# Attention with row maxima: one bank and 512 score columns per exponential, three banks for scores by key, four for scores by query

## Chip, cores and metric

One NeuronCore of a Trainium2 chip runs the whole program. The metric is device time in microseconds (us) of one execution. The profile is of one execution; its span is 2486.1 us, and that execution took 2487.8 us in all.

## What is computed

The reference is one small hybrid network over 2 sequences of 1024 tokens with 128 channels. In order: a wide attention with low-rank updates, an expert layer, a narrow attention (16 heads of 8 channels), an expert layer, a narrow attention over a window, then twice an attention with an expert layer behind it, with a recurrent mixing layer between the two. The change touches three of these parts, in which a softmax subtracts a true row maximum. The first (the window stage here) is

```python
for start in range(0, S, W):                       # W = 128
    scores = einsum('bhqd,bhkd->bhqk', wq, wk) * scale   # wk, wv: keys 0..end
    scores = where(mask, neg, scores)
    attn = softmax(scores, axis=-1)
    outs.append(einsum('bhqk,bhkd->bhqd', attn, wv))
```

and the other two (the causal blocks) are

```python
att = einsum('bhqk' of q, k) / sqrt(hd)
att = where(causal, att, -inf)
att = softmax(att, axis=-1)
y = einsum('bhqk,bhkd->bhqd', att, v)
```

each with 16 heads of 8 channels over 1024 tokens and 2 sequences. (In the first, the mask is counted from key 0 in every block, so the query at place r of a block sees keys 0 to r alone: one tile of 128 keys for all queries.) The narrow attention before them (the clipped one) needs no maximum.

## The kernel before

`four_heads` (L540) runs all four narrow attentions. It takes four heads at a time (8 groups `g` for 2 sequences of 16 heads) and, inside a group, units `(side, kt, c0)`: 512 queries of one side against 128 keys, of which queries before `c0` are cut off by causality. A causal block has 12 units per group: on side 0 widths 512, 384, 256, 128 (kt 0 to 3), on side 1 five of width 512 (kt 0 to 4), then 384, 256, 128. The window stage has 2 units per group, each 512 wide. The argument `use_max` is true for the window stage and the two blocks, and false for the clipped attention.

Per unit, TensorE computes *scores by key* (keys on partitions, queries in columns; `cols`, L681) into PSUM, ScalarE takes the exponential into `probs` (L878, or L874 for a unit at most 256 wide), GpSimd cuts the diagonal (L906), and TensorE multiplies with the values (`values`, L706, two units later: LAG) into bank 7, which ScalarE evicts at the end of a side (L826). The four heads sit in two row groups of the array: heads 0 and 2 on partitions 0 to 63, heads 1 and 3 on 64 to 127, so matmuls of heads i and i+1 run beside each other.

The row maxima come from a second computation, *scores by query* (`score_pair`, L723; mask matmuls L747), which VectorE reduces (`tensor_reduce`, L949). These are the row jobs: 38 per group in a block, issued two at a time. Their maxima are split into three bf16 parts (L849 to L851), turned by TensorE (L785), and loaded by DMA as extra rows of the q stack (L641), so that scores by key come out with the maximum subtracted. The jobs of a group run during the group before it.

PSUM has 8 banks of 512 fp32 columns. With `use_max`: scores by key have banks 0 to 3 as two pairs (`pairs = 2`). One *visit* is two banks, one head in each, 2 x (512 - c0) columns, and one exponential reads it. `cols` of visit n waits until the exponential of visit n-2 is done (L690, L691). A unit over 256 wide has two visits (heads 0, 1 and heads 2, 3), any other one. Banks 4, 5, 6 are a ring for row jobs, turns and the final transposes ("divide", L790): job n waits until job n-3 was read (L727), and as row jobs go in pairs, a pair waits for the first job of the pair before it. Bank 7 holds the outputs. Without `use_max` there are three pairs and one ring bank.

TensorE works in order. Each step s of the loop at L803 is: `cols(U, 0)`, side work of place 0, `values(U - 2)`, side work of place 1, `cols(U, 1)` (where the unit has two visits), side work of place 2. `side_jobs` (L484) places the row jobs: `column_costs` (L473) gives each place a cost, and pairs of jobs are spread evenly over the sum of the costs; so they move only if the costs do. Before the first unit of a stage, step 0 holds the row jobs that must come first.

## Time and profile before

| | us |
|---|---|
| device time, median of 3 runs | 2486.44 (2483.86 to 2488.78) |
| the profiled execution | 2487.8 |
| its span | 2486.1 |
| TensorE matmul busy | 2002.9 (81%) |
| VectorE busy | 1605.0 (65%) |
| ScalarE busy | 1411.4 (57%) |
| GpSimd busy | 876.8 (35%) |

The time is the device time of the whole program. The span runs from the first to the last instruction that the profile holds. Busy times are averages over stages that have different limits. The changed stages lie, in the profiled execution, from about 1410 to 1509 us (window stage), 1545 to 1820 us (first block) and 2059 to 2333 us (second block). TensorE's busy time is modelled from its starts, and each run of matmuls is shown with about 0.18 us of pipeline behind its last column.

### The profile page before, as it was taken

The page shows a single profiled execution, that of the slowest core. Times are in us where ns is not written, and L with a number is a line of the kernel's source. Part 1 is how long each engine was busy: PE and PEld are TensorE (multiplying, and loading weights), DVE is VectorE, ACT ScalarE, POOL GpSimd, SP SyncE. Part 2 cuts the span into 40 slices and gives each one's busy share as a digit, 9 for nine tenths or more (in the row PEclk, how much of TensorE's full clock was granted, in tenths as well). Part 3 has the DMA queues.
Part 4 walks back from the last instruction along what each step waited for, and adds up shares of the span by engine and source line. Part 5 has one row for each costly group of instructions (what it writes and reads, how often), then busy time and mean ns, then how long its engine had stood idle before and what let it go on. Part 6 is the DMA issues. An engine that isn't in the chain of part 4 may idle for free. (4 is left out here: it accounts for less than half of the span.)

```text
span 2486.1 us, 37698 instructions
## 1 busy us (share of the span) xinstructions
PE 2002.9 (81%) x13700; PEld 1132.1 (46%) x13700; DVE 1605.0 (65%) x3423; ACT 1411.4 (57%) x2024; POOL 876.8 (35%) x624
## 2 busy tenths in 40 slices
PE   4999999999999944758836786688879744888798
PEld 2666666666666632622322533122247631222367
DVE  5887787887877546651156464788723685888324
ACT  3777776777778643269852244266753152566641
POOL 3887776877768400242201103122200023121100
PEclk8999999999999966969957888599989865899899
DMA  2000000000000040062050121211010002210100
GB/s 78 1 5 1 3 5 1 1 3 5 1 3 1 1 157 16 2 161 59 11 173 1 51 54 59 74 32 32 17 35 1 1 17 66 74 37 17 35 1 18
DMA packets 55936, 81.37 MB, mean 33 GB/s; under 512 B 13434, under 2 KB 21706, under 8 KB 55626
## 3 DMA queue, kind: packets, MB, share of 16 engines
q1 hardware_dynamic: 55754, 78.96, 11.4%
q8 instruction: 112, 1.84, 0.3%
q14 instruction: 70, 0.57, 0.1%
HBM read 58.85 MB, written 19.33 MB: 31 GB/s over the span
## 5 line engine op out<-in xcount | busy, mean ns | idle before, releaser
L878 ACT ACTIVATE probs<-psum_banks 128x1024 f32<-128x1024 f32 (+1 forms) x416 | 384.2, 981 | 254.9 <-PE psum_banks L695 209.1
L1305 POOL TENSOR_SCALAR l0a_rows<-l0a_rows,l0a_rinv 128x1024 f32<-128x1024 f32 x160 | 454.3, 2844 | 188.2 <-DVE l0a_rinv L1267 184.6
L949 DVE TENSOR_REDUCE neg_max<-psum_banks 128x1 f32<-128x512 f32 (+3 forms) x672 | 415.2, 661 | 136.4 <-PE psum_banks L747 107.3
L1255 DVE TENSOR_REDUCE l0a_nmax<-psum_banks 128x1 f32<-128x1024 f32 x256 | 312.4, 1220 | 140.0 <-PE psum_banks L1149 138.1
L1201 ACT ACTIVATE l0a_rows<-psum_banks,l0a_nmax 128x1024 f32<-128x1024 f32 x256 | 285.8, 1116 | 60.8 <-DVE l0a_nmax L1255 59.3
L718 PE MATMUL psum_banks<-probs,v_ones 128*32 128x512 f32 (+3 forms) x2432 | 265.3, 518 | 7.3 <-POOL probs L906 3.7
L1163 PE MATMUL psum_banks<-packed,l0a_rows 128*128 128x128 f32 x2048 | 267.1, 273 | 2.0 <-POOL l0a_rows L1305 0.9
L1148 PE MATMUL psum_banks<-l0a_kh,l0a_qw 128*128 128x512 f32 x512 | 242.7, 474 | 21.6 <-POOL l0a_qw L1294 13.7
L1163 PEld LDWEIGHTS psum_banks<-packed,l0a_rows 128*128 128x128 f32 x2048 | 239.2, 141 | 42.3 <-issue 4.8
L740 PE MATMUL psum_banks<-k_stack,q_stack 56*128 56x128 bf16 (+3 forms) x1024 | 145.0, 336 | 123.6 <-DVE neg_max L949 91.6
L906 POOL TENSOR_SCALAR_AFFINE_SELECT probs<-probs 128x512 f32<-128x512 f32 x192 | 123.2, 647 | 330.4 <-ACT probs L878 279.9
L695 PE MATMUL psum_banks<-q_stack,k_stack 59*128 59x512 bf16 (+7 forms) x1216 | 177.1, 344 | 65.5 <-ACT probs L878 33.5
L1149 PE MATMUL psum_banks<-l0a_kl,l0a_qw 128*128 128x512 f32 x512 | 205.3, 401 | 0.0
L740 PEld LDWEIGHTS psum_banks<-k_stack,q_stack 56*128 56x128 bf16 x1024 | 48.5, 98 | 292.8 <-DVE neg_max L949 257.8
L1148 PEld LDWEIGHTS psum_banks<-l0a_kh,l0a_qw 128*128 128x128 f32 x512 | 97.9, 191 | 144.1 <-ACT l0a_rows L1201 77.1
L1876 DVE SCALAR_TENSOR_TENSOR l1f_y<-psum_banks,rt_g,l1f_y 128x128 f32<-128x128 f32 x256 | 72.1, 344 | 103.5 <-PE psum_banks L1814 103.5
L1222 DVE SCALAR_TENSOR_TENSOR l0a_ts<-psum_banks,l0a_sin 32x512 f32<-32x512 f32 x192 | 131.9, 687 | 4.2
L1838 ACT ACTIVATE l1f_h<-psum_banks 128x512 f32<-128x512 f32 x128 | 75.6, 598 | 102.6 <-PE psum_banks L1800 102.3
L1196 ACT ACTIVATE x_norm<-psum_banks 128x512 f32<-128x512 f32 x128 | 76.1, 595 | 98.0 <-PE psum_banks L1163 97.8
L695 PEld LDWEIGHTS psum_banks<-q_stack,k_stack 59*128 59x128 bf16 (+1 forms) x1216 | 50.4, 95 | 177.2 <-ACT probs L878 111.1
L433 POOL TENSOR_SCALAR l1f_y<-x_res,ln_mv,ln_rstd 128x128 f32<-128x128 f32 x32 | 25.9, 820 | 297.9 <-DVE ln_rstd L404 297.9
L1175 PE MATMUL psum_banks<-x_norm,l0a_v 128*64 128x512 f32 x512 | 124.0, 604 | 6.0 <-ACT l0a_ot L1206 6.0
(292 smaller groups left out, 3361.2 us busy)
## 6 DMA issues: line engine op xcount, KB each, us to landing
q_stack<-q_parts SPq DMA_DIRECT2D x116, 96.0 KB
k_stack<-k_eight SPq DMA_DIRECT2D x28, 224.0 KB
qkv<-in_l0f_w SPq DMA_DIRECT2D x6, 1024.0 KB, 5.5
k_eight<-parts SPq DMA_DIRECT2D x22, 256.0 KB
moe_b<-in_l0f_b SPq DMA_DIRECT2D x32, 128.0 KB, 3.6
k_stack<-k_eight SPq DMA_DIRECT2D x16, 256.0 KB
l1f_w<-in_l1f_w SPq DMA_DIRECT2D x16, 256.0 KB
k_eight<-first_parts SPq DMA_DIRECT2D x14, 256.0 KB
```

The source lines that it names most:

```text
L695: m = pe.matmul(PS[:, bank, to], S.Kst[stack(i), slot(g, i), kt * P:(kt + 1) * P], S.Qst[stack(i), slot(g, i), side * HALF + c0:(side + 1) ...
L718: m = pe.matmul(PS[32 * i:32 * (i + 1), 7, c0:HALF], S.Vx[:, NT * b + kt, h0 + i, :], S.Pt[:, U % PBUFS, i, c0:HALF], start=kt == 0, stop= ...
L740: last[heads] = pe.matmul(bank[:, at:at + k1 - k0], S.Qst[rows, slot(g, i), jq * P:(jq + 1) * P], S.Kst[rows, slot(g, i), k0:k1], start=fi ...
L878: act.activation(S.Pt[:, U % PBUFS, 2 * half:2 * half + 2, c0:HALF], PS[:, bank:bank + 2, c0:HALF], ACT.Exp).then_inc(exp_done, 1)
L949: dve.tensor_reduce(out, scores, AX, ALU.max, negate=True).then_inc(job_read, 1)
L1148: pe.matmul(scores(s)[:, c0:c0 + HALF], q, R.Kh[:, b, c0:c0 + HALF], start=True, stop=False)
L1149: m = pe.matmul(scores(s)[:, c0:c0 + HALF], q, R.Kl[:, b, c0:c0 + HALF], start=False, stop=True)
L1163: m = pe.transpose(PS[:, 4 + a, jj * P:(jj + 1) * P], R.Pr[:, (NT * ps + 2 * jj + a) % RING, kt * P:(kt + 1) * P], S.ident[:])
L1201: act.activation(R.Pr[:, s % RING, :], scores(s), ACT.Exp, bias=R.nmax4[:, s % 4:s % 4 + 1], accum_out=R.rsum4[:, s % 4:s % 4 + 1]).then_i ...
L1222: ins = dve.scalar_tensor_tensor(R.t_sin[to, u % 3, :], PS[src, bank_of(job), :], scale_of(job), R.sinT[src, job[2] % 2 * HALF:(job[2] % 2 ...
L1255: dve.tensor_reduce(R.nmax4[:, s % 4:s % 4 + 1], scores(s), AX, ALU.max, negate=True).then_inc(max_done, 1)
L1305: rows_divided.mark(pool.tensor_scalar(R.Pr[:, s % RING, :], R.Pr[:, s % RING, :], R.rinv4[:, s % 4:s % 4 + 1], None, ALU.mult))
```

## The change

With `use_max`, scores by key now take banks 0, 1, 2 one at a time, and the ring has banks 3, 4, 5, 6. A visit is now one bank with two heads of one row group (0 and 2, or 1 and 3) side by side in it, up to 256 queries each, so at most 512 columns, and one exponential reads it. `visits_of` lists them: a 512-wide unit has four visits (queries 0 to 255 of heads 0, 2; the same of heads 1, 3; then queries 256 to 511 of each), a 384-wide unit two of 512 columns and two of 256, a 256-wide unit two of 512, a 128-wide unit two of 256. TensorE issues two visits at once, so that the two row groups still work beside each other: `cols(U, v0, v1)` of visits n and n+1 waits for the exponential of visit n-2 (`exp_done` at n-1, for three banks). The first matmul in a bank has start set, the second head's does not. The eviction of the outputs by ScalarE stands behind the first visit of a unit, as it did before. `column_costs` follows the new visits: a 384-wide unit has costs 512 before and 256 after the values, where it had 384 and 384. Without `use_max` nothing changes.

```diff
--- before.py
+++ after.py
@@ -470,14 +470,22 @@
             [(kind, (i,), j) for kind, j in (("full", 4), ("full", 5), ("three", 6), ("full", 6), ("full", 7), ("tail", 7)) for i in range(4)])
 
 
+def visits_of(unit, use_max):
+
+    c0, half = unit[2], HALF // 2
+    if not use_max:
+        return [((0, 1, 2, 3), c0, HALF)] if HALF - c0 <= half else [((0, 1), c0, HALF), ((2, 3), c0, HALF)]
+    cuts = list(range(c0, HALF, half)) + [HALF]
+    return [(heads, q0, q1) for q0, q1 in zip(cuts, cuts[1:]) for heads in ((0, 2), (1, 3))]
+
+
 def column_costs(units):
 
     shape_change = 460
     costs = []
     for side, kt, c0 in units:
-        w = HALF - c0
-        cols = [2 * w, 0] if w <= HALF // 2 else [w, w]
-        costs.append((cols[0], 4 * w + shape_change, cols[1]))
+        streamed = [q1 - q0 for _, q0, q1 in visits_of((side, kt, c0), True)]
+        costs.append((sum(streamed[:2]), 4 * (HALF - c0) + shape_change, sum(streamed[2:])))
     return costs
 
 
@@ -554,7 +562,7 @@
     turn_at = {e: k for k, e in enumerate(turns)}
     first, second = row_jobs(nk)
     last_rows = {e: number["rows", e[1], (second if second and e[2][-1] else first)[-1]] for e in turns}
-    pairs, ring = (2, (4, 5, 6)) if use_max else (3, (6,))
+    in_flight, ring = (3, (3, 4, 5, 6)) if use_max else (3, (6,))
     products_of, rows_of_stack, per_batch = (56, 59, 160) if use_max else (64, 64, 176)
     parts_of_q = ((0, 3), (24, 3), (48, 1)) if use_max else ((0, 3), (24, 3), (48, 2))
     per_group = 16 * 2 * (1 + len(parts_of_q))
@@ -586,14 +594,20 @@
 
         return 16 * sum(transfers_of_c(f) for f in turns[:turn_at[e] + 1] if f[1] % SLOTS == e[1] % SLOTS)
 
-    def narrow(U):
-
-
-        return HALF - units[U % nu][2] <= HALF // 2
+    def pieces(U):
+        return visits_of(units[U % nu], use_max)
 
     visits = [0]
     for U in range(total):
-        visits.append(visits[-1] + (1 if narrow(U) else 2))
+        visits.append(visits[-1] + len(pieces(U)))
+
+    def scores_of(n, visit):
+        heads, q0, q1 = visit
+        w = q1 - q0
+        if use_max:
+            return {i: PS[:, n % in_flight, k * w:(k + 1) * w] for k, i in enumerate(heads)}
+        return {i: PS[:, 2 * (n % in_flight) + i % 2, q0:q1] if len(heads) == 2 else
+                PS[:, 2 * (n % in_flight) + i % 2, i // 2 * w:(i // 2 + 1) * w] for i in heads}
 
     with phase(S, 28) as (block, sems):
         (cols_ready, exp_done, masked, pv_done, evicted, job_ready, job_read, split_done, c_split, c_copied,
@@ -678,30 +692,33 @@
 
         @block.tensor
         def _(pe):
-            def cols(U, h):
-                (g, u), n = divmod(U, nu), visits[U] + h
-                side, kt, c0 = units[u]
-                if h == 0 and u == 0:
+            def cols(U, v0, v1):
+                (g, u), n = divmod(U, nu), visits[U] + v0
+                side, kt, _ = units[u]
+                at_once = [(scores_of(visits[U] + v, pieces(U)[v]), pieces(U)[v]) for v in range(v0, v1)]
+                if v0 == 0 and u == 0:
                     pe.wait_ge(loaded[g % SLOTS], per_group * (g // SLOTS + 1))
-                if h == 0 and use_max and kt == 0:
+                if v0 == 0 and use_max and kt == 0:
                     pe.wait_ge(c_loaded[g % SLOTS], c_landed(next(e for e in turns if e[1] == g and side in e[2])))
                     if U == 0:
                         pe.wait_ge(ones_set, 32)
-                if n >= pairs:
-                    pe.wait_ge(exp_done, n - pairs + 1)
-                for i in range(2 * h, 4 if narrow(U) else 2 * h + 2):
-                    bank = 2 * (n % pairs) + i % 2
-                    to = slice(i // 2 * (HALF - c0), (i // 2 + 1) * (HALF - c0)) if narrow(U) else slice(c0, HALF)
-                    m = pe.matmul(PS[:, bank, to], S.Kst[stack(i), slot(g, i), kt * P:(kt + 1) * P],
-                                  S.Qst[stack(i), slot(g, i), side * HALF + c0:(side + 1) * HALF], start=True,
-                                  stop=tri != "window", skip_group_check=True)
+                if n + v1 - v0 > in_flight:
+                    pe.wait_ge(exp_done, n + v1 - v0 - in_flight)
+                last = {}
+                for k in range(len(at_once[0][1][0])):
+                    for v, (to, (heads, q0, q1)) in enumerate(at_once):
+                        i = heads[k]
+                        last[v] = pe.matmul(to[i], S.Kst[stack(i), slot(g, i), kt * P:(kt + 1) * P],
+                                            S.Qst[stack(i), slot(g, i), side * HALF + q0:side * HALF + q1],
+                                            start=k == 0 or not use_max, stop=tri != "window", skip_group_check=True)
                 for r in range(2 if tri == "window" else 0):
-                    for i in range(2 * h, 2 * h + 2):
-                        rows = stack(i, 64)
-                        m = pe.matmul(PS[:, 2 * (n % pairs) + i % 2, :].rearrange("p (n c) -> p n c", c=P), S.behind[rows, r, :],
-                                      S.before[rows, r, :].unsqueeze(1).to_broadcast([64, 4, P]), start=False, stop=r == 1,
-                                      skip_group_check=True)
-                m.then_inc(cols_ready, 1)
+                    for v, (to, (heads, q0, q1)) in enumerate(at_once):
+                        rows, bank = stack(heads[0], 64), PS[:, (n + v) % in_flight, 0:2 * (q1 - q0)]
+                        last[v] = pe.matmul(bank.rearrange("p (n c) -> p n c", c=P), S.behind[rows, r, :],
+                                            S.before[rows, r, :].unsqueeze(1).to_broadcast([64, 2 * (q1 - q0) // P, P]),
+                                            start=False, stop=r == 1, skip_group_check=True)
+                for v in last:
+                    last[v].then_inc(cols_ready, 1)
 
             def values(U):
                 g, u = divmod(U, nu)
@@ -802,8 +819,10 @@
 
             for s, places in enumerate(steps):
                 U = s - 1
-                if 0 <= U < total:
-                    cols(U, 0)
+                once = 2 if use_max else 1
+                of_step = range(0, len(pieces(U)) if 0 <= U < total else 0, once)
+                for v in of_step[:1]:
+                    cols(U, v, v + once)
                 side_work(places[0])
                 if use_max and 0 <= U - LAG < total:
                     values(U - LAG)
@@ -811,8 +830,8 @@
                     values(U - LAG - 1)
                     values(U - LAG)
                 side_work(places[1])
-                if 0 <= U < total and not narrow(U):
-                    cols(U, 1)
+                for v in of_step[1:]:
+                    cols(U, v, v + once)
                 side_work(places[2])
 
         def evict(eng, V):
@@ -862,21 +881,26 @@
                 U = s - 1
                 if use_max and U in second_batch:
                     parts(second_batch[U])
-                for half in range(1 if U < total and narrow(U) else 2):
+                for v, visit in enumerate(pieces(U)) if U < total else [(0, None)]:
                     if U < total:
-                        side, kt, c0 = units[U % nu]
-                        if U >= PBUFS and half == 0:
+                        heads, q0, q1 = visit
+                        if U >= PBUFS and v == 0:
                             act.wait_ge(pv_done, U - PBUFS + 1)
-                        n = visits[U] + half
+                        n = visits[U] + v
                         act.wait_ge(cols_ready, n + 1)
-                        bank = 2 * (n % pairs)
-                        if narrow(U):
-                            act.activation(S.Pt[:, U % PBUFS, :, c0:HALF].rearrange("p (h a) c -> p a h c", a=2),
-                                           PS[:, bank:bank + 2, 0:2 * (HALF - c0)].rearrange("p a (h c) -> p a h c", h=2),
+                        w, bank = q1 - q0, 2 * (n % in_flight)
+                        if use_max:
+                            act.activation(S.Pt[:, U % PBUFS, heads[0]:heads[-1] + 1:2, q0:q1],
+                                           PS[:, n % in_flight, 0:2 * w].rearrange("p (h c) -> p h c", c=w),
                                            ACT.Exp).then_inc(exp_done, 1)
-                            continue
-                        act.activation(S.Pt[:, U % PBUFS, 2 * half:2 * half + 2, c0:HALF], PS[:, bank:bank + 2, c0:HALF], ACT.Exp).then_inc(exp_done, 1)
-                    if use_max and half == 0 and 0 <= U - LAG < total:
+                        elif len(heads) == 4:
+                            act.activation(S.Pt[:, U % PBUFS, :, q0:HALF].rearrange("p (h a) c -> p a h c", a=2),
+                                           PS[:, bank:bank + 2, 0:2 * w].rearrange("p a (h c) -> p a h c", h=2),
+                                           ACT.Exp).then_inc(exp_done, 1)
+                        else:
+                            act.activation(S.Pt[:, U % PBUFS, heads[0]:heads[1] + 1, q0:HALF], PS[:, bank:bank + 2, q0:HALF],
+                                           ACT.Exp).then_inc(exp_done, 1)
+                    if use_max and v == 0 and 0 <= U - LAG < total:
                         evict(act, U - LAG)
 
         @block.gpsimd
```

## Rows read from the trace of the kernel before

**Rows 1.** the profile page, costliest groups of instructions: the two readers of score banks.

```profile
L878 ACT ACTIVATE probs<-psum_banks 128x1024 f32<-128x1024 f32 (+1 forms) x416 | 384.2, 981 | 254.9 <-PE psum_banks L695 209.1
L949 DVE TENSOR_REDUCE neg_max<-psum_banks 128x1 f32<-128x512 f32 (+3 forms) x672 | 415.2, 661 | 136.4 <-PE psum_banks L747 107.3
```

**Rows 2.** busy time by stretches: four groups; a block's start; window unit pair; a pause.

```profile
core 0: us, PE busy (x) PEld busy (x) DVE busy (x) ACT busy (x) POOL busy (x), PEclk, DMA share, GB/s
1660.03:1773.43 113.40, 95.99 (x982) 33.32 (x980) 98.35 (x177) 74.71 (x89) 24.77 (x53) 1.00 0.13 28
1550.91:1571.04 20.13, 8.99 (x60) 3.42 (x61) 14.93 (x29) 0.00 (x0) 3.51 (x4) 0.50 0.07 16
1571.04:1631.68 60.64, 43.55 (x334) 13.88 (x334) 46.58 (x83) 26.89 (x30) 15.03 (x18) 0.68 0.33 87
1470.44:1479.53 9.09, 9.08 (x98) 3.88 (x98) 7.12 (x20) 5.29 (x7) 0.00 (x0) 1.00 0.22 61
1250.00:1260.00 10.00, 5.84 (x25) 4.76 (x25) 4.89 (x23) 3.37 (x6) 0.00 (x0) 0.50 0.15 24
```

**Rows 3.** timeline of ScalarE in the second block: evictions five groups apart (start, us).

```profile
2156.12 0.61 ACT L826 ACTIVATE o_sum<-psum_banks 128x512 f32<-128x512 f32 x1
2297.86 0.60 ACT L826 ACTIVATE o_sum<-psum_banks 128x512 f32<-128x512 f32 x1
```

**Rows 4.** waits, longest in total, in one group, 1745.08 to 1773.43 us.

```profile
PE psum_banks L740 <- DVE neg_max L949: 3.1, 6, 0.7
PE psum_banks L695 <- ACT probs L878: 0.9, 2, 0.5
```

**Rows 5.** timeline of TensorE in the same group (start us, us, what).

```profile
1750.47 0.64 PE L718 MATMUL psum_banks<-probs,v_ones 128*32 128x256 f32 x8
...
1756.39 0.39 PE L695 MATMUL psum_banks<-q_stack,k_stack 59*128 59x512 bf16 x2
1757.13 0.39 PE L740 MATMUL psum_banks<-k_stack,q_stack 56*128 56x512 bf16 x2 [0.34 <-DVE neg_max L949]
...
1757.56 1.07 PE L718 MATMUL psum_banks<-probs,v_ones 128*32 128x512 f32 x8
1758.56 0.39 PE L740 MATMUL psum_banks<-k_stack,q_stack 56*128 56x512 bf16 x2
...
1758.90 0.60 PE L695 MATMUL psum_banks<-q_stack,k_stack 59*128 59x512 bf16 x4
1759.93 0.40 PE L740 MATMUL psum_banks<-k_stack,q_stack 56*128 56x128 bf16 x8 [0.44 <-DVE neg_max L949]
```

**Rows 6.** timeline of ScalarE: exponentials in a row, and one after a wait.

```profile
1754.00 3.91 ACT L878 ACTIVATE probs<-psum_banks 128x1024 f32<-128x1024 f32 x4
1759.32 1.94 ACT L878 ACTIVATE probs<-psum_banks 128x1024 f32<-128x1024 f32 x2 [1.42 <-PE psum_banks L695]
```

**Rows 7.** groups by shape in the same group: an exponential of 512 columns.

```profile
L874 ACT ACTIVATE probs<-psum_banks 128x512 f32<-128x512 f32 x2 | 1.2, 597 | 1.8 <-PE psum_banks L695 1.8
```

**Rows 8.** timeline, last group of the second block: an exponential's end, and TensorE behind it.

```profile
2310.94 2.64 ACT L878 ACTIVATE probs<-psum_banks 128x1024 f32<-128x1024 f32 x3 [1.24 <-PE psum_banks L695]
...
2312.02 0.34 PE L695 MATMUL psum_banks<-q_stack,k_stack 59*128 59x384 bf16 x2 [0.28 <-ACT probs L878]
```

**Rows 9.** timeline of TensorE: both ends of the second block's last stretch.

```profile
2300.73 0.39 PE L695 MATMUL psum_banks<-q_stack,k_stack 59*128 59x512 bf16 x2
2329.38 0.28 PE L695 MATMUL psum_banks<-q_stack,k_stack 59*128 59x128 bf16 x4
```

**Rows 10.** timeline, window stage: VectorE at its start, then one unit's end.

```profile
1418.32 1.29 DVE L949 TENSOR_REDUCE neg_max<-psum_banks 128x4 f32<-128x512 f32 x2 [0.95 <-PE psum_banks L747]
...
1478.66 0.40 PE L695 MATMUL psum_banks<-q_stack,k_stack 59*128 59x512 bf16 x2
1479.53 1.02 ACT L878 ACTIVATE probs<-psum_banks 128x1024 f32<-128x1024 f32 x1 [0.86 <-PE psum_banks L701]
...
1480.19 0.39 PE L695 MATMUL psum_banks<-q_stack,k_stack 59*128 59x512 bf16 x2
```

## Prediction

> **What bounds the kernel now.** I first read the costliest groups: the exponentials wait for scores by key, the row reductions for scores by query [rows 1]. So no reader of a score bank is the bound by itself. Then the busy time by stretches. In a block's even part the kernel repeats every 28.35 us (the evictions stand 141.74 us apart for five groups [rows 3]), and there TensorE is busy 85%, VectorE 87%, ScalarE 66% of the time at a granted clock of 1.00 [rows 2]. Two engines near 86% that wait for each other are a handshake. The waits of one such group name it: TensorE waits 3.1 us in 6 pieces for VectorE to free a ring bank, and 0.9 us in 2 pieces for ScalarE [rows 4]. A block's start runs at 0.50 and 0.68 of the clock; before the first scores by key VectorE works 14.93 of 20.13 us, and the next 60.64 us hold 46.58 us of its work [rows 2]. The window stage is different: TensorE is busy 9.08 of 9.09 us [rows 2].
>
> So the steps to price are four: the even groups, the last group of a block (no row jobs left), the window stage, and the starts.
>
> **TensorE's own work in an even group.** 28.35 us less the waits of 3.1 and 0.9 us [rows 4], and less the modelled tail in front of each wait. The tail: matmuls at 1756.39 are shown for 0.39 us, but where nothing waits, as at 1758.56, the scores by key start 0.34 us later although two mask matmuls lie between; 512 columns take about 0.21 us, so 0.18 us is tail [rows 5]. With one more short wait there are 9, or 1.6 us. Own work: 28.35 - 4.2 - 1.6, or 22.5 us. The change leaves this sum: a 512-wide unit has 8 matmuls of 256 columns in place of 4 of 512, two at a time, the same columns. Twice the weight loads lie beside matmuls, as they do in the 4-head units of today; I take 0, with 0 to 0.5 us per group as bounds, by the widest gap between 0.60 us shown for x4 and twice 0.21 plus the tail [rows 5].
>
> **What goes.** With four ring banks a pair of row jobs waits for the pair before the last, 1.25 us or more earlier than now. The 3.1 us per group go. VectorE's 24.6 us per group (98.35 over 4) [rows 2] would be late next, from below that period.
>
> **What comes.** With three banks taken two at a time, `cols` of a pair of visits waits for the first exponential of the pair just before it. That loop has three pieces. Scores by key issued at 1758.90 start an exponential at 1759.32: 0.42 us [rows 5, 6]. An exponential of 512 columns takes 0.60 us [rows 7]. TensorE goes on 0.06 us after an exponential ends (2310.94 + 1.02 is 2311.96, then 2312.02) [rows 8]; I take 0.08. In sum 1.10 us from one `cols` to the next, unless other TensorE work of that length lies between. Before, the wait was for a visit issued two earlier, and second half and next first half went back to back: x4 in 0.60 us at 1758.90 [rows 5]. The long work (values, 1.00 us from 1757.56 to 1758.56 [rows 5], and most row jobs) lies between first and second half, so there the loop is covered. Between a second half and the next unit's first half there is mostly nothing but 0.21 us of its own.
>
> Added wait per unit of a group, with what lies between taken off:
> - side 1, kt 2: the divide lies between, 0.9 us own: wait 0.2.
> - kt 3 and kt 4: 1.10 - 0.21, 0.9 each.
> - kt 5 (384 wide): the second half is 2 x 128 columns, so an exponential of 256; from 597 ns at 512 and 963 ns steps at 1024 (3.91 us for four, less one of 1.02, over 3 [rows 6, 7]) I take 0.38 us; loop 0.84, less 0.11: wait 0.7.
> - kt 6, kt 7 and the two narrow units of side 0: one pair of visits, values between: 0.
> - side 0, kt 0: a pair of row jobs moves here (below): 0.6 after, nothing before.
> - side 0, kt 1: 0.6 before its second half (values of 128 columns are short, under 0.43 us); behind it ScalarE still has the eviction and one exponential to do, which stand between: 0.42 + 0.60 + 0.55 + 0.54 + 0.35 + 0.08, or 2.55 us from the unit's start to the next unit: 0.95 more.
> - side 1, kt 0: values of 256 columns (about 0.58 us, shown as 0.64 [rows 5]) and a pair of jobs almost cover the first loop: 0.1; behind it 0.9.
> - side 1, kt 1: again the eviction: 0.2 and 1.35.
> Sum 7.4 us. The new period is 22.5 + 7.4, 29.9; adding the steps unit by unit gives 29.83. Against 28.35 that is +1.48 us. There are 5 such groups per block [rows 3], 2 blocks: **+14.8 us**. An error of 0.1 us in the loop is 0.9 us per group, so bounds of +0.5 and +2.5 per group.
>
> The moved pair: by the new costs, the ninth pair of a group's 19 comes nearest to the end of unit (0, 0) and goes from in front of the values of (0, 1) to just before its first scores. It changes no own work and fills a wait; counted above. VectorE and GpSimd get nothing new. SP's queue keeps its order: the DMA of the turned maxima may land up to 0.5 us after it is wanted, since units kt 6 and 7 get faster; in the high bound.
>
> **ScalarE.** An extra exponential costs 2 x 0.54 - 0.963, 0.12 us. There are 20 more per group and 16 such groups, 32 more in the window stage, 352 in all, 42 us of ScalarE. In even groups it has 9.7 us idle of 28.35 (18.7 busy, from 74.71 over 4 [rows 2]) and the 2.4 us stay hidden. The Trainium skill ("ScalarE: Activation LUTs", section "What ACT_TABLE_LOAD costs") gives a fixed 186 ns per ACTIVATE with immediate operands and an overlap of about 93 ns back to back; by it an extra one costs 0.09 us and 33 us in all, which would lie on the path only if ScalarE were the bound throughout.
>
> **The last stretch.** From 2300.73 to 2329.38 us, 28.65 us [rows 9], two row pairs are left and ScalarE sets the pace: 2 x 0.963 us for a 512-wide unit. After, such a unit takes values 1.00, own 0.21, loop 1.10: 2.31. Added up over the 16 units: 3.1 + 2.3 + 2.1 + 1.2 + 0.9, then 2.2 + 2.45 + 1.8 + 0.9 + 2.2 + 2.7, then 3 x 2.3 + 2.0 + 1.2, about 32.1. **+3.5 us per block, +7** (bounds 2 and 14).
>
> **The window stage.** TensorE is the bound. From a second half to the next first half it now goes 1.53 us (1478.66 to 1480.19), with a divide and a turn, and 1.33 without the turn. Scores to exponential is 0.87 us here (mask matmuls) [rows 10], so the loop is 0.87 + 0.60 + 0.08, 1.55 to 1.6. Wait 0.17 us on average, 16 units: **+2.7** (0 to 5).
>
> **The starts.** There row pairs follow one another with nothing between, and each wait on the ring shows: in the window stage 0.95 us in front of the second pair, and so on for about seven [rows 10]. TensorE needs about 1.3 us per pair at the low clock and VectorE 1.29, so of some 7 us I take **-4** (-7 to -2; a q stack landing late would eat the rest). In a block 5.2 us of the first 20.13 are idle VectorE [rows 2]; -3.5 of that. In the next 60.64 us VectorE idles 14 us; most of it is TensorE's doubled work at the low clock and stays, new waits come: another -3.5. **-14 for both blocks** (-4 to -28).
>
> **Sum.** 14.8 + 7 + 2.7 - 4 - 14 = +6.5 us. On the profiled execution's 2487.8 that is 2494.3; it lies 1.4 above the median of 2486.44, so the median becomes 2493. Bounds: 5 + 4 + 0 - 7 - 28 = -26, and 25 + 14 + 5 - 2 - 4 = +38.
>
> **Rivals.** (a) *The freed ring wins.* The engine that decides is VectorE: if at the starts, where both ends of the handshake wait (14 us idle of 60.64 [rows 2]), four banks let it run on, each block gains 12 instead of 7 us, and if the loop is 1.0 us and not 1.10 the even groups cost 0.6 and not 1.48. Then 6 + 5 + 1 - 6 - 24 = -18: 2468 to 2480, 2476 as its middle. It decides from a net of under 0 at an even group cost of 0.8 us. For it: 3.1 us of VectorE waits against 0.9 of ScalarE waits today [rows 4]. Against: the loop's pieces are all in rows.
> (b) *It cancels.* The even groups and the last ones cost about 16, starts and ring give 16: 2482 to 2491.
> (c) *The clock falls.* In side 1's first two units TensorE would be busy some 60% for 5 us; in a pause of the kernel with 5.84 busy of 10 us the granted clock was 0.50, the lower level of 1.2 GHz; the even groups have 1.00 [rows 2]. If each even group lost the upper level for one unit with 1.00 us of values and 1 us other own work, that is +2 us, 10 groups, +20, and 2513; for two units 2533. The Trainium skill ("TensorE: Matmul & The Clock Gate", section "A second HAM failure mode: psum-queue depth-cycling") says that TensorE, idling briefly between groups as it cycles its PSUM banks, can have its clock go back and forth between both levels. In the even groups today the trace shows none [rows 2]; no row has them with the longer waits.
>
> **Chances.** Forecast (2488 to 2505) 0.43; (a) 0.23; (b) 0.19; (c) 0.15. A difference of 0.2%, 5 us, is what a measurement of this kernel can tell from none. Faster by more: 0.23. Within: 0.27, which is (b) and the forecast's lower edge. Slower: 0.50. The range that leaves 2 in 10 out is 2474 to 2518; the forecast's own is 2488 to 2505.
>
> **What would show it.** In the trace after: waits of scores by key for an exponential at 7 us per group in place of 0.9, waits of row jobs for VectorE near 0; evictions in the second block 29.8 us apart per group; an exponential of 512 columns at 0.60 us, back to back 0.54; the first scores by key of a block 3.5 us sooner after its first reduction than 20.1 us; window unit pairs 9.4 us apart. It is wrong if the evictions are 28 us apart or less (the loop is shorter or covered), or if the clock shows less than 1.00 in even groups.

## The result

| | before | after |
|---|---|---|
| device time, median of 8 runs each, us | 2487.74 (2482.07 to 2492.88) | 2504.19 (2499.67 to 2515.02) |
| ratio | | 1.0074 [1.0052, 1.0096] |
| profiled execution / its span, us | 2487.8 / 2486.1 | 2514.77 / 2512.4 |
| mean granted clock of the profiled execution | 0.893 | 0.888 |

The change costs 16.5 us. The profiled execution of the kernel after is 10.6 us above its own median, so stage times below add up to more than 16.5. Its eight runs differ in the clock: the two of 2515 us had a mean of 0.887 and 0.888, the others of 2500 to 2509 us 0.891 to 0.897.

Where the 26.3 us between the two profiled spans lie (stretches end at the same event in both traces):

| stretch | before | after | difference | forecast |
|---|---|---|---|---|
| window stage, last eviction | 1509.11 | 1511.82 | +2.7 | +2.7 - 4 |
| first block: first reduction to eviction of group 1, side 0 | 89.2 | 77.75 | -11.5 | -7 |
| its five even groups | 141.75 | 154.2 | +12.4 | +7.4 |
| its last stretch, to the loads that follow it | 36.7 | 50.7 | +14.0 | +3.5 |
| second block: start | 91.4 | 78.0 | -13.4 | -7 |
| its five even groups | 141.74 | 154.1 | +12.4 | +7.4 |
| its last stretch, to the last eviction | 33.9 | 42.8 | +9.0 | +3.5 |

The rest, some +0.7 us, lies between the stages (+1.5 and +3.2) and behind the last (-4.1). The costliest groups of the page after, which answer to [rows 1]: the exponentials now all read one bank (576 of 512 columns, 597 ns on average, and 128 of 256, 387 ns; the row puts both under one form and gives their mean, 559 ns), and TensorE waits 84.5 us for them.

```profile
L893 ACT ACTIVATE probs<-psum_banks 128x512 f32<-128x512 f32 x704 | 355.9, 559 | 256.3 <-PE psum_banks L711 213.9
L973 DVE TENSOR_REDUCE neg_max<-psum_banks 128x1 f32<-128x512 f32 (+3 forms) x672 | 407.3, 659 | 150.0 <-PE psum_banks L764 91.1
L711 PE MATMUL psum_banks<-q_stack,k_stack 59*128 59x256 bf16 (+5 forms) x1792 | 191.1, 292 | 136.2 <-ACT probs L893 84.5
```

Busy time by stretches of the kernel after, as in [rows 2]: four even groups of the first block, five of the second, the last stretch of each block, a pair of window units.

```profile
core 0: us, PE busy (x) PEld busy (x) DVE busy (x) ACT busy (x) POOL busy (x), PEclk, DMA share, GB/s
1663.77:1787.07 123.30, 101.75 (x1110) 36.92 (x1108) 96.65 (x177) 83.03 (x169) 24.90 (x52) 0.94 0.11 24
2165.16:2319.26 154.10, 127.38 (x1387) 46.11 (x1385) 120.74 (x220) 103.79 (x211) 31.11 (x65) 0.94 0.12 26
1787.07:1835.50 48.43, 38.18 (x313) 10.48 (x313) 8.34 (x18) 33.34 (x68) 8.77 (x17) 0.79 0.01 2
2319.26:2362.70 43.44, 32.93 (x315) 9.32 (x313) 8.30 (x18) 33.42 (x68) 8.77 (x17) 0.92 0.01 2
1474.08:1483.42 9.34, 9.01 (x111) 4.27 (x109) 7.21 (x19) 5.53 (x10) 0.00 (x0) 1.00 0.20 58
```

An even group takes 30.82 us (154.10 over 5) against 28.35, VectorE is down from 87% to 78% busy, and the clock of these groups, 1.00 before, is 0.94. The last stretches, which ran at 1.00 before, show 0.79 and 0.92.

The waits of one even group of the kernel after (2196.29 to 2227.07 us; as [rows 4]: total us, times, longest us):

```profile
ACT probs L893 <- PE psum_banks L711: 9.8, 11, 1.9
PE psum_banks L711 <- ACT probs L893: 5.0, 8, 1.1
DVE neg_max L973 <- PE psum_banks L757: 4.2, 4, 1.3
```

TensorE's wait for VectorE, 3.1 us in 6 pieces before, has no row; that for ScalarE went from 0.9 to 5.0 us. The timeline of TensorE at the switch from one side to the next in that group:

```profile
2196.45 0.39 PE L711 MATMUL psum_banks<-q_stack,k_stack 59*128 59x256 bf16 x4
2197.91 0.61 PE L711 MATMUL psum_banks<-q_stack,k_stack 59*128 59x256 bf16 x4 [1.08 <-ACT probs L893]
...
2198.88 1.93 PE L735 MATMUL psum_banks<-probs,v_ones 128*32 128x512 f32 x8
...
2202.87 1.06 PE L735 MATMUL psum_banks<-probs,v_ones 128*32 128x512 f32 x8
...
2204.21 0.38 PE L711 MATMUL psum_banks<-q_stack,k_stack 59*128 59x256 bf16 x4
2205.28 0.39 PE L711 MATMUL psum_banks<-q_stack,k_stack 59*128 59x256 bf16 x4 [0.69 <-ACT probs L893]
```

ScalarE beside it, with the eviction in front of the exponentials:

```profile
2196.29 0.59 ACT L845 ACTIVATE o_sum<-psum_banks 128x512 f32<-128x512 f32 x1
2196.76 1.58 ACT L893 ACTIVATE probs<-psum_banks 128x512 f32<-128x512 f32 x3
```

And the granted clock, microsecond by microsecond (us, TensorE busy, clock, DMA share, GB/s):

```profile
2196.00:2197.00 1.00, 0.77 (x10) 1.00 0.00 0
2197.00:2198.00 1.00, 0.09 (x2) 0.86 0.00 0
2198.00:2199.00 1.00, 1.00 (x10) 0.50 0.00 0
2199.00:2200.00 1.00, 1.00 (x8) 0.50 0.00 0
2200.00:2201.00 1.00, 1.00 (x6) 0.50 0.00 0
2201.00:2202.00 1.00, 1.00 (x10) 0.94 0.00 0
2202.00:2203.00 1.00, 0.90 (x16) 1.00 0.00 0
```

Two things are to be seen. Where nothing lies between two `cols`, they stand 1.07 us apart (2204.21 to 2205.28): the loop of the prediction, forecast at 1.10. And at the side switch, where the eviction stands in ScalarE's queue, TensorE does almost nothing from 2196.84 to 2197.91; the clock falls to the lower level, 1.2 GHz, for some 3.4 us (2197.7 to 2201.1), and the values take 1.93 us instead of 1.06. All ten even groups have this fall once, at this place.

### The profile page after: what moved, and what is told of

It is laid out like the page before. It is cut to its first block and busy times, and to the rows that moved or that the text cites. A ratio compares the mean times of both kernels' runs of the same rounds, so it can differ in the third digit from the quotient of the medians.

```text
span 2512.4 us, 39202 instructions
## 1 busy us (share of the span) xinstructions
PE 2027.2 (81%) x14276; PEld 1158.3 (46%) x14276; DVE 1598.0 (64%) x3423; ACT 1448.2 (58%) x2376; POOL 878.6 (35%) x624
## 5 line engine op out<-in xcount | busy, mean ns | idle before, releaser
L893 ACT ACTIVATE probs<-psum_banks 128x512 f32<-128x512 f32 x704 | 355.9, 559 | 256.3 <-PE psum_banks L711 213.9
L973 DVE TENSOR_REDUCE neg_max<-psum_banks 128x1 f32<-128x512 f32 (+3 forms) x672 | 407.3, 659 | 150.0 <-PE psum_banks L764 91.1
L711 PE MATMUL psum_banks<-q_stack,k_stack 59*128 59x256 bf16 (+5 forms) x1792 | 191.1, 292 | 136.2 <-ACT probs L893 84.5
L735 PE MATMUL psum_banks<-probs,v_ones 128*32 128x512 f32 (+3 forms) x2432 | 278.6, 542 | 4.4 <-POOL probs L930 3.7
L711 PEld LDWEIGHTS psum_banks<-q_stack,k_stack 59*128 59x128 bf16 (+1 forms) x1792 | 62.2, 96 | 275.0 <-ACT probs L893 150.1
L757 PEld LDWEIGHTS psum_banks<-k_stack,q_stack 56*128 56x128 bf16 x1024 | 50.7, 102 | 206.1 <-DVE neg_max L973 144.4
```

The lines of the kernel that those rows point to most:

```text
L711: last[v] = pe.matmul(to[i], S.Kst[stack(i), slot(g, i), kt * P:(kt + 1) * P], S.Qst[stack(i), slot(g, i), side * HALF + q0:side * HALF + q1],
L735: m = pe.matmul(PS[32 * i:32 * (i + 1), 7, c0:HALF], S.Vx[:, NT * b + kt, h0 + i, :], S.Pt[:, U % PBUFS, i, c0:HALF], start=kt == 0, stop= ...
L757: last[heads] = pe.matmul(bank[:, at:at + k1 - k0], S.Qst[rows, slot(g, i), jq * P:(jq + 1) * P], S.Kst[rows, slot(g, i), k0:k1], start=fi ...
L893: act.activation(S.Pt[:, U % PBUFS, heads[0]:heads[-1] + 1:2, q0:q1], PS[:, n % in_flight, 0:2 * w].rearrange("p (h c) -> p h c", c=w), AC ...
L973: dve.tensor_reduce(out, scores, AX, ALU.max, negate=True).then_inc(job_read, 1)
```

## The experiments

The theory: three banks taken two at a time make the 1.07 us loop (even groups slower by about a microsecond), the ring of four banks gives time back at the starts, and the pauses let the clock fall (rival c). The main rival: it is the 352 added exponentials on ScalarE, with the eviction between them.

**Both bank counts.** The ring was `in_flight, ring = (3, (3, 4, 5, 6))`.

```diff
-    in_flight, ring = (3, (3, 4, 5, 6)) if use_max else (3, (6,))
+    in_flight, ring = (4, (4, 5, 6)) if use_max else (3, (6,))   # e1_four_three
+    in_flight, ring = (3, (4, 5, 6)) if use_max else (3, (6,))   # e2_three_three
```

> The changed kernel with four banks for scores by key (still one bank, 512 columns and one exponential per visit) and three in the ring: the split of the exponentials alone. Theory (three banks taken two at a time make TensorE wait for the exponential just issued, and these waits let the clock fall once a group): the wait now is for a visit of the pair before the last, so the even groups go back to 28.3 to 28.8 us, waits of scores by key for an exponential to 1 us or less, waits of row jobs for VectorE to about 3 us, granted clock 1.00, and the whole to 2485 to 2495 us. Rival (the 352 extra exponentials of 0.12 us cost the time): the even groups stay at 30 us or more and the whole at 2500 us or more.

> The changed kernel with three banks for scores by key and three in the ring (bank 3 left empty): the loss of look-ahead without the fourth ring bank. Theory: the waits for VectorE come back beside those for ScalarE; even groups 31.5 to 32.5 us, the starts of the stages 3 to 5 us longer each, the whole 2515 to 2530 us. Rival (the fourth ring bank gives nothing once TensorE waits for ScalarE): the same as the changed kernel, 2504 us and 30.8 us per group.

Measured: e1 2506.66 us, 1.0083 [1.0066, 1.0100]; e2 2553.80 us, 1.0256 [1.0232, 1.0279]. Both missed their times upwards; e2's even groups, 32.3 us on average, are in their range. Against three and three, the fourth bank of the ring is worth 49.6 us and the fourth bank for scores by key 47.1 us: the change moves a bank between two uses that need it about equally. What the ring bank gives is seen at the starts: from the first reduction to the eviction of group 1, side 0, e1 takes 91.9 and 90.6 us in the two blocks, the kernel before 89.2 and 91.4, the kernel after 77.8 and 78.0. That e1 isn't back near 2488 refutes the theory as the only cause. Its clock stays at 1.00 in even groups and its group takes 29.49 us (2166.83 to 2314.26 is five): no loop and no fallen clock, yet 1.1 us more than before. ScalarE's timeline at its side switch has eleven operations without a rest, then one of 0.28 us:

```profile
2223.29 2.64 ACT L893 ACTIVATE probs<-psum_banks 128x512 f32<-128x512 f32 x5 [1.84 <-PE psum_banks L711]
2225.80 0.62 ACT L845 ACTIVATE o_sum<-psum_banks 128x512 f32<-128x512 f32 x1
2226.28 2.59 ACT L893 ACTIVATE probs<-psum_banks 128x512 f32<-128x512 f32 x5
2229.15 1.08 ACT L893 ACTIVATE probs<-psum_banks 128x512 f32<-128x512 f32 x2 [0.28 <-PE psum_banks L711]
```

and TensorE waits for VectorE again, 3.0 us in 6 pieces of the group 2216 to 2246.5:

```profile
PE psum_banks L757 <- DVE neg_max L973: 3.0, 6, 0.7
```

e1 also has the pause of the kernel after, as long and at the same place, in front of the scores behind the eviction:

```profile
2226.97 0.39 PE L711 MATMUL psum_banks<-q_stack,k_stack 59*128 59x256 bf16 x4 [1.08 <-ACT probs L893]
```

Its clock stays at 1.00 there and in all ten even groups. So a pause of 1.08 us doesn't by itself bring the clock down.

**The clock.** Matmuls whose results nobody reads fill TensorE's pauses in the two blocks, at nine places of a group (e3) or at the side switch alone (e13).

```diff
+                if use_max and U:
+                    fill(FILL.get((units[u][:2], v0), 0), g)
                 if n + v1 - v0 > in_flight:
                     pe.wait_ge(exp_done, n + v1 - v0 - in_flight)
+            # e3_fill: matmuls per (side, kt), visit; k matmuls of 512 columns into the next ring bank
+            {((1, 2), 0): 5, ((1, 3), 0): 1, ((1, 4), 0): 3, ((1, 5), 0): 3, ((1, 6), 0): 2,
+             ((0, 1), 0): 1, ((0, 1), 2): 2, ((0, 2), 0): 3, ((1, 1), 0): 3}
+            # e13_fill_one: {((1, 2), 0): 5}
```

> The changed kernel with 1 to 5 matmuls of 512 columns whose result nobody reads, into the free ring bank, in front of those scores by key of the two blocks that wait for an exponential. They take the place of idle time and remove no wait. Theory (the idle time lets the clock fall): granted clock 1.00 in even groups (0.94 in the changed kernel), no values at 1.9 us, even groups 29.2 to 29.6 us instead of 30.8, the last stretch of the first block 37 to 39 us instead of 48; the whole 2480 to 2492 us. Rival (the clock falls for another reason, or only the loop counts): even groups at 30.8 us or more, the whole 2504 us or more.

> The changed kernel with five unread matmuls of 512 columns in a single place of each group of the two blocks: in front of the first scores of side 1, kt 2, where TensorE pauses for 1.1 us behind an eviction. Theory (this one pause lets the clock fall each group): clock 1.00 in even groups, 29.3 to 29.6 us per group as with all places filled, the whole 2488 to 2496 us. Rival (the lower activity of the whole group is the cause): the clock still falls, at other places, 30.5 us or more per group.

Measured: e3 2489.26 us (10 runs), 0.9998 [0.9988, 1.0009]. More work on TensorE makes the kernel 14.9 us faster than the change without it; the even groups take 29.4 us (29.46 on average in the second block) at a clock of 1.00, and the last stretch 40.2 us in both blocks, where 37 to 39 was expected of the first. The second block's:

```profile
2295.97:2336.14 40.17, 37.84 (x352) 12.16 (x350) 8.30 (x18) 32.81 (x67) 8.73 (x17) 1.00 0.01 2
```

So the fallen clock costs 30.82 - 29.46, or 1.4 us per even group; in the last stretch, counted to the last eviction, it costs 42.84 - 40.17, or 2.7 us, in the second block and 47.92 - 40.17, or 7.7 us, in the first. With the clock held, that stretch is still 6.3 us longer than before (33.86):

```profile
2297.86:2331.72 33.86, 29.31 (x261) 8.25 (x261) 7.69 (x17) 28.36 (x35) 8.63 (x17) 1.00 0.01 2
```

e1 splits the 6.3. It has the same exponentials, four key banks and a clock of 1.00, and takes 36.65 us (evictions at 2314.26 and 2350.91; 36.5 in the first block). From there to e3 it is 3.5 us, for three key banks in place of four; from the kernel before to e1 2.8 us, for the new cut of the units with its added exponentials.

e13: 2497.80 us, 1.0044 [1.0025, 1.0064]. One filled pause gives only 6.4 of the 14.9 us, less than expected, and what happened is the recorded rival: the clock still falls, at another place. Of the five even groups of its second block one takes 29.4 us, three 30.6 and one 32.2, and the clock over all five is 0.94 again. In a group of 30.6 us the filled switch (2247 to 2251) now has 1.00, and the clock falls at the other switch of sides, 8 us earlier; granted clock by the microsecond there, and TensorE's pauses in front:

```profile
2238.00:2239.00 1.00, 0.31 (x4) 0.75 0.66 117
2239.00:2240.00 1.00, 1.00 (x8) 0.50 0.09 18
2240.00:2241.00 1.00, 1.00 (x8) 0.50 0.00 0
2241.00:2242.00 1.00, 1.00 (x8) 0.55 0.00 0
```

```profile
2237.44 0.29 PE L727 MATMUL psum_banks<-q_stack,k_stack 59*128 59x128 bf16 x4 [0.39 <-ACT probs L910]
2237.56 0.38 PE L773 MATMUL psum_banks<-k_stack,q_stack 56*128 56x512 bf16 x2
2238.69 0.61 PE L727 MATMUL psum_banks<-q_stack,k_stack 59*128 59x256 bf16 x4 [0.75 <-ACT probs L910]
```

So the 1.08 us pause is where the clock falls in the kernel after, but with it filled the clock falls at a pause of 0.75 us in seven of the ten even groups. The same pause of 0.75 us leaves it at 1.00 in e13's group from 2187 to 2217 (at 2209.39), and in the kernel after (at 2219.85). What besides the pauses decides is not shown.

**The eviction.** In a unit of four visits it goes behind the third exponential instead of the first (e5); the same with four key banks (e7); or it goes to VectorE, behind the first row jobs of its unit (e9).

```diff
-                    if use_max and v == 0 and 0 <= U - LAG < total:
+                    if use_max and v == (2 if visit and len(pieces(U)) == 4 else 0) and 0 <= U - LAG < total:   # e5, e7
                         evict(act, U - LAG)
+    in_flight, ring = (4, (4, 5, 6)) if use_max else (3, (6,))   # e7 only
+                eng.tensor_copy(S.Oc[:, out % 2, :], PS[:, 7, :]).then_inc(evicted, 1)   # e9, eng is VectorE
```

> The changed kernel with ScalarE's eviction of the outputs behind the third visit of a four-visit unit, and not the first. Theory (behind the eviction the second unit of a side waits 2.6 us for its next scores, and the pause of 1.1 us there is what lets the clock fall): the exponential that TensorE waits for comes 0.5 us sooner at both side switches, the clock stays at 1.00 in even groups, and the group goes from 30.75 to 28.5 to 29.2 us; the whole 2472 to 2488 us. Rival (ScalarE is simply full at the side switch, its work of 10 exponentials and an eviction in a row being the bound, so their order doesn't count): 30.2 us or more per group, 2498 us or more.

> The kernel with four banks by key and three in the ring and one bank per exponential, which had 29.48 us per group, with the eviction behind the third visit. Theory of order (both of its long waits, 0.97 and 1.08 us, stand behind an eviction that lies between two exponentials): 28.4 to 28.7 us per group, the whole 2486 to 2494 us. Rival (the extra exponentials, 0.12 us each, some 9 of them in the stretch at each group's side switch in which ScalarE never rests): 29.3 us or more, 2503 us or more.

> The changed kernel with the eviction of the outputs on VectorE (0.69 us each) and not on ScalarE, in the three stages with maxima, behind the row jobs of place 0. It takes the eviction out of ScalarE's chain at the side switch altogether. Theory (ScalarE is the bound there, by its count of exponentials and the eviction): 28.6 to 29.2 us per group, clock 1.00, the whole 2475 to 2488 us; if only the order on ScalarE counted, the same as with the eviction behind the third visit. Rival (VectorE, now 26 us busy per group, delays the eviction behind its row jobs and values wait for it): 30 us or more, 2500 us or more.

Measured: e5 2488.29 us (10 runs), 1.0006 [0.9992, 1.0019]; its even groups take 28.7 to 29.0 us at a clock of 1.00, but for the last of each block (30.5 and 30.2 us at 0.94), and TensorE's waits in one (2173.07 to 2201.80) are 4.2 us with none over 0.7:

```profile
PE psum_banks L711 <- ACT probs L893: 4.2, 8, 0.7
```

The place of one instruction of 0.6 us is worth 15.9 us, nearly the whole loss: the long pause goes, and with it, in eight of ten groups, the fall of the clock (28.72 us is below the 29.4 of e3, which held the clock up but left the eviction where it was). e9: 2485.50 us, 0.9992 [0.9978, 1.0005]; six of its ten even groups take 28.5 us, the other four 29.9 to 30.1 us at a clock of 0.94, where 1.00 was expected. In e5 and e9 the groups with a fall and those without show the same two pauses of 0.69 us in front of it (e5 at 2257.17 and 2259.39, and at 2228.45 and 2230.67). e7: 2516.44 us, 1.0126 [1.0104, 1.0147], 29.57 us per group against 29.49 of e1: with four key banks and 512-column exponentials the order doesn't matter, as the rival has it. It is 9.8 us above e1 all the same, and the cause stays open. In the profiled executions, whose spans are 11.3 us apart, 8.4 lie between the two blocks (4.5) and behind the second (3.9), in stages whose code is the same in both. Such stages differ from one profiled execution to the next: from the first block's last eviction to the second block's first reduction the runs here take 248.2 to 253.4 us.

**The exponentials alone.** The kernel before, each exponential cut into two of one bank (the units at most 256 wide likewise, not printed here).

```diff
-                        act.activation(S.Pt[:, U % PBUFS, 2 * half:2 * half + 2, c0:HALF], PS[:, bank:bank + 2, c0:HALF], ACT.Exp).then_inc(exp_done, 1)
+                            act.activation(S.Pt[:, U % PBUFS, 2 * half, c0:HALF], PS[:, bank, c0:HALF], ACT.Exp)
+                            act.activation(S.Pt[:, U % PBUFS, 2 * half + 1, c0:HALF], PS[:, bank + 1, c0:HALF], ACT.Exp).then_inc(exp_done, 1)
```

> The kernel before, with each exponential of the three stages cut in two that read one bank each, and the bank pair handed back after the second: the same number of exponentials as the changed kernel, and nothing else of it. Theory (352 extra exponentials at 0.12 us; they show only where ScalarE is the bound, at the side switch of a group and in the last group): 29.1 to 29.6 us per even group, the whole 2500 to 2512 us, as far from before as the split with four and three banks was. Rival (hidden, and what that kernel lost came from its banks or its waits): 28.4 us or less, 2486 to 2492 us.

Measured: 2497.19 us, 1.0048 [1.0030, 1.0065], with 28.59 us per even group (2164.11 to 2278.49 is four). The added instructions cost some 10 us, but only 0.25 us per even group, 2.5 us in ten; expected was more, 29.1 us or above per group and 2500 us or above. The profiled spans are 11.4 us apart: besides the 2.5 us, 3.2 lie in the two last stretches (the second has one fall of the clock), 2.3 in the starts, and 3.4 elsewhere. From here to e1 another 9 us come in that neither bank count nor number of exponentials explains, and they lie in the even groups: 29.49 against 28.60 us, ten times. e1 differs from e10 in that a unit is cut by queries and not by heads, in twice as many matmuls of half the columns with their weight loads, in banks that are handed over one by one to ScalarE, and in the place of one pair of row jobs. Which of these it is was not tried.

**The row jobs.** e4 puts all row jobs of a unit in its last place, between its last scores and the next unit's first; e8 has e5's eviction, and in the blocks half of the row jobs behind the values and half behind the second scores; e11 is e9 with e8's placing; e12 is the kernel before with it.

```diff
-        costs.append((sum(streamed[:2]), 4 * (HALF - c0) + shape_change, sum(streamed[2:])))
+        costs.append((0, 0, sum(streamed) + 4 * (HALF - c0) + shape_change))   # e4
+        whole = sum(streamed) + 4 * (HALF - c0) + shape_change                 # e8, e11, blocks only
+        costs.append((0, whole // 2, whole // 2) if len(streamed) == 4 else (0, whole, 0))
```

> The changed kernel with the row jobs of a step all put behind its last scores by key (place 2), by the costs (0, 0, sum). Theory: a pair or two of row jobs (0.35 to 0.75 us) then lies in the loop of 1.07 us between a unit's second scores and the next unit's first, which is where TensorE waits; even groups 26 to 28 us, with VectorE's 24.6 as the floor, clock 1.00, the whole 2445 to 2470 us. Rival (VectorE starves between bunched jobs, or the bunch waits for the ring): even groups at 28.4 us or more.

> The changed kernel with the eviction behind the third visit, and in the two blocks the row jobs of a four-visit unit half behind the values and half behind the second scores by key (window stage as in the changed kernel). Theory: one pair lies in each loop and VectorE is fed evenly: even groups 26.5 to 27.5 us, clock 1.00, the whole 2450 to 2468 us, the fastest so far. Rival (TensorE's and ScalarE's waits only trade places): 28.2 us or more, 2480 us or more.

> The kernel with evenly placed row jobs (27.77 us per group, 2477 us), but with the eviction on VectorE and not behind ScalarE's third visit. Theory (at the side switch ScalarE is the bound, and VectorE has room at 26 of 27.8 us): 27.0 to 27.6 us per group, 2466 to 2476 us. Rival (VectorE is now near its own bound and hands its banks back late): 27.8 us or more, 2478 us or more.

> The kernel before, with only the placing of the row jobs changed: in the two blocks half behind the values, half behind the second scores by key. Theory (the place between second and first scores is worth filling only where three banks make a wait there; with a ring of three each pair still waits for the pair before it): 28.3 us or more per group, 2485 to 2500 us. Rival (the placing alone is the gain): 27.8 us or less, 2480 us or less.

| | us | ratio | most even groups, us |
|---|---|---|---|
| e4 | 2486.62 | 0.9996 [0.9983, 1.0008] | 28.26 |
| e8 | 2477.01 (7 runs) | 0.9958 [0.9942, 0.9974] | 27.77 |
| e11 | 2471.28 | 0.9937 [0.9918, 0.9956] | 27.77 |
| e12 | 2507.49 | 1.0087 [1.0066, 1.0107] | 29.24 |

e4 missed its 2445 to 2470. Row jobs between two `cols` cover the loop (waits of 2.1 us in the group 2203.36 to 2231.61 instead of 5.0), but placed in bunches they wait for VectorE (1.9 us in 3 pieces), although the ring has four banks:

```profile
PE psum_banks L711 <- ACT probs L893: 2.1, 8, 0.4
PE psum_banks L757 <- DVE neg_max L973: 1.9, 3, 1.0
```

and a pair of window units takes 10.16 us instead of 9.34. e8 spreads them and leaves the window stage as it is; it missed its 2450 to 2468 us and 26.5 to 27.5 us per group. e11, with VectorE evicting, is the fastest kernel here, 16 us below the kernel before and 33 below the change. Its even groups at a clock of 1.00:

```profile
2163.49:2274.56 111.07, 95.38 (x1112) 36.73 (x1110) 98.93 (x186) 79.60 (x161) 24.82 (x52) 1.00 0.11 27
```

VectorE is busy 89% there, TensorE 86%. The period hoped for, 27.0 to 27.6, was not reached, and its last stretches take 40.3 and 44.9 us (the second at a clock of 0.81) against 33.9 before. The same placing makes the kernel before some 20 us slower (e12), more than was expected, so here it pays only with the change's banks.

## Why the prediction came out as it did

The direction and its reason held; 16.5 us came instead of 6.5. But the clock shows 0.94 in even groups, and less than 1.00 there was one of the two signs by which the prediction wanted to be called wrong. Its sum had no term for the clock, which cost some 24 us: ten times 1.4 in even groups, 2.7 and 7.7 in the last stretches.

- *TensorE's waits move from VectorE to ScalarE.* Right: 3.1 us to no row, 0.9 to 5.0 us, where it named 7.
- *The loop, 0.42 + 0.60 + 0.08.* Right: 1.07 us where nothing covers it.
- *Even groups, 28.35 to 29.83.* With the clock held, e3 has 29.4, 0.4 below; the kernel itself 30.82, 1.0 above. The price was about right, but not all of it is the loop's: e5, with the loop and the eviction moved, has 28.72, and e1, without the loop, has 29.49. Rival (c), given 0.15, came on top in every even group: priced at +2, it measures +1.4. It falls at another place than the rival said: not in side 1's first two units for want of work, but in the one pause of 1.08 us at the side switch, and such a pause isn't enough by itself (e1). The prediction had the eviction in that loop ("0.42 + 0.60 + 0.55 + 0.54 + 0.35 + 0.08") and priced its length without asking what the pause does to the clock. The Trainium skill ("TensorE: Matmul & The Clock Gate", section "A second HAM failure mode: psum-queue depth-cycling") has a TensorE that idles briefly between groups, as it cycles its PSUM banks, go back and forth between both clock levels. The trace after agrees, with 0.50 for some 3.4 us of each 30.8, and e3 and e5 show it from two sides, by filling the pauses and, in eight of ten groups, by shortening the longest.
- *The last stretch, +3.5 per block.* The step that failed most: +9.0 and +14.0. The loop itself was right: three key banks in place of four make 3.5 us there (e1 to e3; e3 also has the unread matmuls). The sum had no term for the 2.8 us of the new cut and its added exponentials (before to e1), nor for the clock, 2.7 us in the second block and 7.7 in the first. (Its list adds up to 31.95 us, not 32.1.) In the first block the clock, by two microseconds at a time, falls three times, behind a stretch of little work each:
```profile
1787.00:1789.00 2.00, 0.69 (x8) 0.78 0.01 4
1789.00:1791.00 2.00, 2.00 (x14) 0.50 0.00 0
...
1807.00:1809.00 2.00, 0.71 (x14) 0.90 0.00 0
1809.00:1811.00 2.00, 1.93 (x12) 0.50 0.00 0
...
1817.00:1819.00 2.00, 0.89 (x16) 0.96 0.00 0
1819.00:1821.00 2.00, 1.65 (x12) 0.50 0.00 0
```

- *The added exponentials "stay hidden".* True of even groups (+0.25 us each in e10), false for the kernel: e10 is some 10 us above the kernel before, 3.2 of them in the last stretches. No term stood for it.
- *The starts, -7 per block.* Mis-sized, to the good side: -11.5 and -13.4. The first piece was exact: the first scores by key come 16.50 us after the first reduction (1555.13 to 1571.63) against 20.13, -3.6 for -3.5. In the remaining part rival (a) was right: TensorE's waits for VectorE from the first reduction to the first even group fall from 26.6 us in 33 pieces to 9.8 in 18, and with three ring banks (e1) the starts are as long as before. The clock of these stretches rose too, from 0.67 to 0.71 and from 0.62 to 0.73; how much of the gain is the clock's is not shown. Before, then after:

```profile
PE psum_banks L740 <- DVE neg_max L949: 26.6, 33, 2.0
PE psum_banks L757 <- DVE neg_max L973: 9.8, 18, 1.0
```

- *Window stage, +2.7.* The pair of units takes 9.34 us against 9.09 (forecast 9.4) and the stage ends 2.7 us later. Half of the -4 at its start came: the first eviction is 26.7 us behind the first reduction against 28.8 before. But the stage begins 1.1 us later, and from the first to the last eviction it takes 3.6 us more, not 2.7.

By terms, in the profiled executions: forecast +14.8 + 7 + 2.7 - 4 - 14 = +6.5; measured +24.8 + 23 + 2.7 - 24.9 = +25.6, and 0.7 between the stages. Errors of +10 (even groups) and +16 (last stretches) met one of -7 (starts, window included); that the median was off by no more than 10 is in part luck.

Open: what decides whether the clock falls at a pause (e1 against the kernel after, e5 and e9 from group to group), and so why the first block's last stretch loses it three times and the second's twice (0.79 against 0.92); the 9 us from e10 to e1; the 9.8 us from e1 to e7.

## What to carry to other kernels

Count banks by how they are handed over, not by how many there are: three banks taken two at a time give no look-ahead past the pair just issued, and a loop of scores, exponential and semaphores (1.07 us here) shows wherever no other TensorE work lies between. Then ask of each new pause what it does to the clock and not only how long it is: here the clock that fell at a pause of a microsecond cost 1.4 us per group, more than the pause, while in e1 the same pause cost no clock. So look at the granted clock microsecond by microsecond, and in several groups, before and after a repair. A cheap repair can lie in the reader's queue: moving a 0.6 us eviction two exponentials back gave nearly the whole loss back, and row jobs placed into the new gaps turned the change into a gain.

## What the runs showed that was not expected

- One pause of 1.08 us in a group of 30.8 us comes with some 3.4 us at 1.2 GHz, and with that pause filled the fall moves, in most groups, to another one of 0.75 us (e13). The same pause of 1.08 us in e1 leaves the clock at 1.00. Filling the pauses with unread matmuls gained 14.9 us.
- The same instruction isn't equally long in every kernel: the eviction of 128x512 took 0.59 us in the kernel after and 0.62 to 0.64 in e1, e7 and e10, which have their scores by key in banks 0 to 3 and one bank per exponential, and the exponential of 512 columns 597 ns against 612 to 622 (645 in e10's units of 256). An activation of the same size in a later stage took 598 or 599 ns in all of them. The cause was not tried.
- The same placing of row jobs helps or harms by the bank layout: -11.3 us from e5 to e8 and -14.2 from e9 to e11, some +20 in the kernel before.
